# A one-core decoder layer: the order of the pipelined attention steps is changed on four engines

## Time and profile before

| | us |
|---|---|
| median of 3 runs | 1018.22 |
| lowest, highest | 1016.80, 1019.21 |
| profiled execution, its own time | 1016.69 |
| span of the profile, first to last instruction | 1014.6 |
| mean granted TensorE clock | 0.973 |
| PE busy | 938.4 (92%) |
| DVE busy | 665.9 (66%) |
| ACT busy | 604.4 (60%) |
| POOL busy | 370.4 (37%) |

### The profile page before, as it was taken

One profiled execution on the slowest core, in us unless ns is written; L12 is line 12 of the kernel. 1 busy time (PEld: TensorE's weight loads), 2 busy tenths in 40 slices (PEclk: granted clock), 3 DMA queues, 4 the chain that ended last, 5 costly groups with the idle time before them and its releaser, 6 DMA issues.

```text
span 1014.6 us, 29842 instructions
## 1 busy us (share of the span) xinstructions
PE 938.4 (92%) x10845; PEld 827.4 (82%) x10845; DVE 665.9 (66%) x1985; ACT 604.4 (60%) x1528; POOL 370.4 (37%) x631
## 2 busy tenths in 40 slices
PE   6899999999999999999968999999999999999960
PEld 4788888888888888788757899999999999999950
DVE  3576776767867777677744567575565775575546
ACT  3556656656566565665535576575665765675536
POOL 0225445454444544445532432222322222223223
PEclk7999999999999999999979999999999999999985
DMA  8102141111111211113011344343535342522328
GB/s 273 48 33 65 44 147 40 55 64 54 55 34 54 64 54 49 35 58 115 29 37 34 56 113 125 53 125 61 126 46 139 54 125 42 145 43 43 47 37 331
DMA packets 57362, 79.91 MB, mean 79 GB/s; under 512 B 5728, under 2 KB 46048, under 8 KB 57120
## 3 DMA queue, kind: packets, MB, share of 16 engines
q1 hardware_dynamic: 41504, 58.50, 18.0%
q0 software_dynamic: 13536, 18.16, 10.5%
q10 hardware_dynamic: 2208, 1.73, 0.6%
HBM read 52.10 MB, written 29.71 MB: 81 GB/s over the span
## 4 chain that ended last, share of the span: by engine, by line
PE 72%; DVE 8%; ACT 7%; issue 6%; POOL 5%; DMA 1%; ACTq 0%; DVEq 0%; SPq 0%; POOLq 0%
PE bank L820 15%; PE bank L834 10%; PE bank L511 9%; PE bank L836 5%; PE bank L673 4%; PE bank L573 3%; PE bank L718 3%; PE bank L626 3%; POOL sent_rows L1707 3%; PE bank L598 3%; PE bank L647 2%; PE bank L593 2%; ACT h_f L1161 2%; PE bank L694 2%; ACT last_out L1237 1%
## 5 line engine op out<-in xcount | busy, mean ns | idle before, releaser
L820 PE MATMUL bank<-xs_hi,w_both 128*128 128x256 f32 x1152 | 241.8, 287 | 0.0
L1155 ACT ACTIVATE h_parts<-bank,bfc_s 128x256 fp32r<-128x256 f32 x288 | 139.6, 485 | 156.1 <-PE bank L820 151.1
L1717 POOL DMA_INDIRECT residual_sum<-y_w,meta_i x72 | 116.7, 1621 | 300.6 <-DVE y_w L1535 276.8
L1493 DVE TENSOR_TENSOR h_parts<-h_f,h_parts 128x256 fp32r<-128x256 f32 x288 | 121.3, 425 | 145.0 <-ACT h_f L1161 140.0
L834 PE MATMUL bank<-w_both,h_parts 128*128 128x512 f32 x544 | 200.0, 398 | 1.1 <-DVE h_parts L1493 1.1
L820 PEld LDWEIGHTS bank<-xs_hi,w_both 128*128 128x128 f32 x1152 | 191.0, 190 | 8.1 <-issue 1.7
L820 PE MATMUL bank<-xs_lo,w_both 128*128 128x256 f32 x576 | 162.7, 282 | 0.0
L836 PE MATMUL bank<-w_both,h_parts 128*128 128x256 f32 x544 | 153.0, 281 | 0.0
L1161 ACT ACTIVATE h_f<-bank,bfc_s 128x256 f32<-128x256 f32 x288 | 138.9, 482 | 3.9 <-DVE h_parts L1493 3.4
L834 PEld LDWEIGHTS bank<-w_both,h_parts 128*128 128x128 f32 x544 | 102.5, 188 | 19.9 <-DVE h_parts L1493 3.5
L820 PEld LDWEIGHTS bank<-xs_lo,w_both 128*128 128x128 f32 x576 | 109.5, 190 | 0.1
(11 more groups left out here) (183 smaller groups left out, 2168.5 us busy)
## 6 DMA issues: line engine op xcount, KB each, us to landing
rows<-sent_rows SPq DMA_DIRECT2D x37, 258.0 KB
xc_raw<-in_turned SPq DMA_DIRECT2D x32, 256.0 KB
w_raw<-in_w_fc SPq DMA_DIRECT2D x8, 1024.0 KB
w_raw<-in_w_proj SPq DMA_DIRECT2D x8, 1024.0 KB
x_t<-in_x SPq DMA_DIRECT2D x32, 128.0 KB, 2.3
residual_sum<-x_row SPq DMA_DIRECT2D x32, 128.0 KB, 1.7
last_in<-residual_sum SPq DMA_DIRECT2D x7, 512.0 KB, 6.9
result<-last_out SPq DMA_DIRECT2D x7, 512.0 KB, 2.7
```

The costliest lines, as they stand in the source:

```text
L820: last = mm(ps_h(g, j), w[:, at:at + P], v[:, k, :], start=(n == 0), stop=(n == 3 * NCH - 1))
L1155: A(h_hi[j % 4][:, :], ps_h(g, j), ACT.Gelu_apprx_tanh, bias=bias)
L1493: V.tensor_tensor(h_lo[j % 4][:, :], h_f[j % 2][:, :], h_hi[j % 4][:, :].bitcast(f32), ALU.subtract).then_inc(s["h_split"], 1)
L1717: G.indirect_dma_start(total, bass.IndirectOffsetOnAxis(meta_i[:, half:half + 1], 0), y_w[:, half, :], None, compute_op=ALU.add)\
```

## The change

No stage is added or removed and the stages themselves are as before; each list is put in another order. What moves:

- PE, even step: `att_proj` ahead of `qx`; `rank` ahead of `ret_values`; `prep_kx` from ahead of `qx` to behind `ret_values`; `max_scores` behind `gn_mean` and `y_back`; `max_turn` of sequence k-1 leaves the end of the step and becomes `max_turn` of k-2 near the start of the odd step.
- PE, odd step: `x1_turn` ahead of `prep_k`; `ret_values` ahead of `att_scores`; `gn_mean` ahead of `rank`; `y_back` ahead of `prep_q`.
- ACT: `y_out` ahead of `att_exp` in odd steps; `kx_out` later in even ones; the copies `x1_T_out` and `max_hi_out` and one `x_high` move from the odd step's start to the even step's end; in the odd step `max_hi_out` of k-1 stands ahead of `v_out`.
- DVE: `max_split` and `pick` of the even step's sequences move into the next odd step; `gn_moments`, `gn_centre` and the first norm stand earlier, `max_twice` later; `x_low` later.
- POOL: `send` stands last in both kinds of step (it stood ahead of `x1_bo_` in even ones and ahead of `gn_rstd` in odd ones); `shares` stands behind `gn_rstd`, once per step (the even step had two, the odd one none).

```diff
@@ PE
                 if not odd:
                     run(ret_scores, At(k))
                     run(att_back, At(k - 3))
                     run(x1_turn, At(k - 1))
+                    run(att_proj, At(k - 3))
+                    run(qx, At(k - 1))
+                    run(att_scores, At(k - 2))
+                    run(rank, At(k - 4))
+                    run(ret_values, At(k))
                     pair_run(prep_kx, k // 2)
-                    run(qx, At(k - 1))
-                    run(att_proj, At(k - 3))
-                    run(att_scores, At(k - 2))
-                    run(ret_values, At(k))
-                    run(rank, At(k - 4))
-                    run(max_scores, At(k - 1))
                     run(gn_mean, At(k))
                     run(y_back, At(k))
+                    run(max_scores, At(k - 1))
                     run(x2_turn, At(k - 3))
                     run(att_values, At(k - 2))
                     run(logits, At(k - 3))
                     run(prep_v, At(k + 1))
                     run(o_turn, At(k - 2))
-                    run(max_turn, At(k - 1))
                 if odd:
                     run(ret_scores, At(k))
                     run(att_back, At(k - 3))
+                    run(max_turn, At(k - 2))
+                    run(x1_turn, At(k - 1))
                     pair_run(prep_k, (k + 1) // 2)
-                    run(x1_turn, At(k - 1))
+                    run(qx, At(k - 1))
                     run(att_proj, At(k - 3))
-                    run(qx, At(k - 1))
+                    run(ret_values, At(k))
                     run(att_scores, At(k - 2))
-                    run(ret_values, At(k))
+                    run(gn_mean, At(k))
                     run(rank, At(k - 4))
+                    run(y_back, At(k))
                     pair_run(prep_q, (k + 1) // 2)
-                    run(gn_mean, At(k))
-                    run(y_back, At(k))
                     run(max_scores, At(k - 1))
...
@@ ACT
                 if not odd:
-                    run(x1_T_out, At(k - 1))
                     if k >= 0:
                         pair_run(x_high, (k + 2) // 2, 0)
                     run(att_back_out, At(k - 3))
-                    pair_run(kx_out, k // 2)
+                    run(x1_T_out, At(k - 1))
                     run(max_out, At(k - 2))
                     run(qx_out, At(k - 1))
...
                     run(y_out, At(k))
+                    pair_run(kx_out, k // 2)
                     run(x2_T_out, At(k - 3))
                     run(o_out, At(k - 2))
                     run(v_out, At(k + 1))
+                    run(x1_T_out, At(k))
+                    if k >= 0:
+                        pair_run(x_high, (k + 2) // 2, 1)
+                    run(max_hi_out, At(k - 1))
                 if odd:
                     run(att_back_out, At(k - 3))
-                    run(x2_again, At(k - 4))
-                    run(max_hi_out, At(k - 2))
-                    run(x1_T_out, At(k - 1))
+                    run(qx_out, At(k - 1))
+                    pair_run(k_out, (k + 1) // 2)
                     run(max_out, At(k - 2))
-                    if k >= 0:
-                        pair_run(x_high, (k + 2) // 2, 1)
-                    pair_run(k_out, (k + 1) // 2)
-                    run(qx_out, At(k - 1))
+                    run(y_out, At(k))
...
-                    run(y_out, At(k))
                     pair_run(q_out, (k + 1) // 2)
+                    run(x2_again, At(k - 4))
                     run(x2_T_out, At(k - 3))
+                    if k < B - 1:
+                        run(x2_again, At(k - 3))
                     run(o_out, At(k - 2))
                     if k == -1:
                         w_high(3)
+                    if k < B - 1:
+                        run(max_hi_out, At(k - 1))
                     run(v_out, At(k + 1))
-                    if k < B - 1:
-                        run(x2_again, At(k - 3))
-                        run(max_hi_out, At(k - 1))
@@ DVE
                 if not odd:
...
+                    run(ln2_stats, At(k - 3))
+                    run(ln2_norm, At(k - 3))
+                    run(put, At(k - 4))
+                    run(gn_moments, At(k))
+                    run(gn_centre, At(k))
                     pair_run(x_low, (k + 2) // 2, 0)
-                    run(ln2_stats, At(k - 3))
-                    run(put, At(k - 4))
-                    run(ln2_norm, At(k - 3))
-                    run(gn_moments, At(k))
                     for r in range(NT):
                         run(att_max, At(k - 1), r)
-                    run(max_twice, At(k - 1))
-                    run(gn_centre, At(k))
                     run(lg_out, At(k - 3))
                     run(ln1_stats, At(k))
+                    run(ln1_sum, At(k))
                     run(att_norm, At(k - 2))
-                    run(ln1_sum, At(k))
-                    run(pick, At(k - 3))
+                    run(max_twice, At(k - 1))
                     run(ln1_norm, At(k))
-                    run(max_split, At(k - 1))
                 if odd:
...
+                    run(max_split, At(k - 2))
+                    run(pick, At(k - 4))
+                    if k >= 0:
+                        pair_run(x_low, (k + 2) // 2, 1)
                     run(ln2_stats, At(k - 3))
                     run(ln2_norm, At(k - 3))
-                    if k >= 0:
-                        pair_run(x_low, (k + 2) // 2, 1)
                     run(gn_moments, At(k))
                     run(put, At(k - 4))
                     run(gn_centre, At(k))
+                    run(ln1_stats, At(k))
                     if k < B - 1:
                         for r in range(NT):
                             run(att_max, At(k - 1), r)
                         run(lg_out, At(k - 3))
-                    run(ln1_stats, At(k))
-                    if k < B - 1:
+                        run(ln1_sum, At(k))
                         run(max_twice, At(k - 1))
-                        run(ln1_sum, At(k))
+                        run(pick, At(k - 3))
                         run(att_norm, At(k - 2))
                         run(ln1_norm, At(k))
                         run(max_split, At(k - 1))
-                        run(pick, At(k - 3))
@@ POOL
                 if k % 2 == 0:
...
+                    run(gn_rstd, At(k))
                     run(shares, At(k - 4))
-                    run(gn_rstd, At(k))
                     run(rstd, At(k), l1rstd[:, :], l1var[:, :], "ln1_var", "ln1_rstd")
+                    run(x1_bo_, At(k))
                     run(send, At(k - 4))
-                    run(x1_bo_, At(k))
-                    run(shares, At(k - 3))
                 else:
                     run(xb_, At(k))
                     run(rstd, At(k - 3), l2rstd[:, :], l2var[:, :], "ln2_var", "ln2_rstd")
-                    run(send, At(k - 4))
                     run(gn_rstd, At(k))
+                    run(shares, At(k - 4))
                     run(rstd, At(k), l1rstd[:, :], l1var[:, :], "ln1_var", "ln1_rstd")
                     run(x1_bo_, At(k))
+                    run(send, At(k - 4))
```

## The result

The changed kernel takes 1006.16 us (median of 3 runs, 1003.73 to 1007.03), the kernel before 1018.22: a ratio of 0.9876, 95% interval 0.9851 to 0.9902. The profiled execution took 1003.73 us, its span is 1001.7 (before 1016.69 and 1014.6). So the span fell by 12.9 us, where 22.8 were forecast.

What follows compares the result with a forecast made beforehand. PE, busy 92%, was taken as the bound: -14.2 - 2.4 - 4.2 - 2.0 = -22.8 us from 1016.69 gives 993.9, plus 1.5 for a median about 995 us; range 986 to 1010, forecast's own 988 to 1001.

Steps and rivals of the forecast that it cites:

- rivals A and B: A (chance 0.16): held PE increments move instead of going, 1004; B (0.08): ACT bounds the even step's start, 1008.
- three signs of being wrong: PE idle over 0.5 us in odd steps; ACT copies waiting on nameless releaser after scatter; time moving under 10 us.
- The odd step's 1.26 us and their two causes: PE's loss before `o_turn` and `max_turn`, from POOL's queue ahead of `gn_rstd` and held increments; all 1.26 us go.
- the 1.33 foretold for both kinds of step: PE's `max_scores` was to take 1.33 us in even steps too, where exponentials had spread it to 1.78.
- The even step: PE's new order: -0.45 us for `max_scores`, +0.46 for a new hole, +0.16 for `ret_decay`.
- The hole for `attT`: New 0.46 us wait of `att_proj` in every even step, as `prep_kx` no longer covers ACT's copies.
- the 0.16 us for `ret_decay`: Even step: the earlier `att_scores` waits for `ret_decay`, losing 0.1 to 0.2 us, taken as 0.16.
- Steps with the weights' split: Four odd steps lose the 0.6 us by which the split's piece delays `ret_decay`: -2.4 us; even ones keep theirs.
- the 1.1 us that `ret_decay` has in hand: In the new odd step `ret_decay` has about 1.1 us before `ret_values`, enough to absorb the split's 0.6 us.
- The end: PE's 4.54 us hole for the last sequence's x1 before the drain: -4.2 us, and -2.0 for the clock behind it.
- the -2.0 us for the clock: With the hole before the drain gone, the clock stays up: -2.0 us for two 4 us stretches behind it.

Runs made afterwards that it cites:

- the copy early: The change with GpSimd's old lists, plus ACT's `x2_again(k - 4)` back behind `att_back_out` in odd steps: 1049.0 us, ratio 1.0318 to the kernel before.

## Why the prediction was right and wrong

The time, 1006.16, lies in the range of 986 to 1010, but 11 us above the forecast and outside its own 988 to 1001. It is near the 1004 and 1008 of rivals A and B, for whose sake the range reached so far, but neither happened, so that the range held is luck: no copy of ACT waits for a nameless releaser in the steady steps after (28 waits for `att_values`, the longest 0.7 us), and the even steps take 14.32 us. Of the prediction's three signs of being wrong one came: PE idle for over 0.5 us in odd steps, those with the split.

*The odd step's 1.26 us and their two causes*: right, and shown. Odd steps fell by 1.43 us; scatter last alone gives 1.30, of which the queue is 0.55 and the held increments 0.75. The last 0.13 comes with the other lists: from start to start `att_scores` takes 1.59 us in place of 1.97, while `max_scores` takes 1.45, not the 1.33 foretold for both kinds of step.

*The even step*: forecast +0.17 (0.46 + 0.16 - 0.45), measured -0.12. The hole for `attT` is there (`att_proj` starts 0.64 us after `x1_turn`, which alone takes 0.14, so 0.50), `max_scores` takes 1.33, but the 0.16 us for `ret_decay` never came, and `att_scores` takes 1.59 us from start to start in place of 1.78. With the odd step a pair gained 1.55, not 1.09, us.

*Steps with the weights' split*: this is the step that failed: "four odd steps lose their 0.6: -2.4 us". The forecast has them at 17.52 - 1.26 - 0.6 = 15.66; they took 17.52 to 19.16. Nothing came of either gain, and two of them lost a dip's 1.6 more. I had counted the 1.1 us that `ret_decay` has in hand, from DVE's list alone, and not read what stands ahead of ACT's piece in the new list, though I had listed `x1_T_out`'s move. Moving the piece alone gives back 14 us, more than the 10.5 by which this stretch was off (in the profile 11.4 there and 2.7 from step 31 on), and the odd steps then take 15.5.

*The end*: forecast -6.2, measured -3.8. The 4.54 us hole of the earlier trace rows is gone (`x1_turn` follows `logits` at 502.11) and the clock is 1.00 from 490 to 520. In its place `max_turn` waits 1.13 us and `att_proj` 1.23 us right behind. And a dip came back at 540, behind PE's idle of 2.62 us for the last exponentials. The kernel before has the same hole, at 552.6, with the clock at 1.00 behind it. Nor does "if the hole is gone the clock should stay up" hold at the first place in every execution: in the second profile of the changed kernel `x1_turn` follows `logits` as well (506.03), and the clock is 0.59 from 508 to 512 and 0.56 from 512 to 516. So the -2.0 us for the clock was mis-sized; with the scatter last alone, and no dip between 490 and 560 us, this stretch takes 510.6 us, against 512.5 and 511.7 in the two profiles of the changed kernel. Whether the other lists cost anything here can't be told from these.

*Steps 0 to 3*: priced at nothing, they cost 3.1 us. No scatter is issued beside them yet, so nothing is gained there, while step 0 takes 10.68 for 8.75 us, with PE's wait of 2.56 us for `ret_decay` and a dip behind it, step 1 14.35 for 13.66, step 2 13.12 for 12.94 and step 3 16.08 for 15.73. Scatter last alone has 8.61, 13.66, 12.95 and 15.73, and the change with GpSimd's old lists 10.91, 14.34, 13.13 and 16.08, so it comes from the lists of PE, ACT and DVE; which of them was not told apart.

The Trainium skill, "TensorE: Matmul & The Clock Gate", section "What's actually happening", has the gate follow recent activity. The trace agrees in that these dips stand behind holes. It also shows that equal holes differ: of four of 1.98 us two were followed by a dip, in the second profile of the same kernel three. A hole's price is then its length, and in some executions 1.6 us more.

## What to carry to other kernels

Try each engine's list alone before all together: here one moved line gave 23 us, and the rest of the rewrite, which suits the steady steps (another 0.23 us a pair), took about half of them back: 9 to 11 us in the eight steps that carry extra work at their end and 3 in the first four. When a list is changed, follow what is appended to the step in rare cases, and ask for each appended instruction what now stands ahead of it and who waits for it on the other engine. And keep a scatter's issue away from the matmul whose result is wanted next.

## What the hardware showed

While POOL issues two indirect DMAs, semaphore increments of PE can come late although PE's next matmuls start on time (before: `logits` at 224.07, `prep_v` at 224.54). An increment is seen here by the copy that waits for it; since the ends of matmuls are modelled, the trace can't tell a late increment from a late end. In the kernel before, the copies behind `att_values` and `logits` start 1.6 and 1.1 us after the modelled ends in the steps with a scatter beside them; with the scatter last alone it is 0.1 and 0.5 us. The copy that waits starts 0.5 to 0.8 us behind the second issue's end in three kernels: 225.20 to 225.77 before, 221.73 to 222.22 with `gn_rstd` first, 230.00 to 230.80 with the copy early; in the last it is `x2_turn` that is late, and DVE stands idle, so neither `att_values` nor a busy DVE is what does it. There PE itself stands still for 0.32 us too, after 6 of the 32 matmuls of `att_values`, and goes on at 230.46, behind the second issue. Five plain stores, issued for 2.81 us at the same place, hold nothing. What stays open is the mechanism, and why the even steps' scatters, in all kernels, stand beside increments that land on time, and why that of `x2_turn` in the kernel before, 0.2 us into the first issue, does too.
